# First attention: lead of the maxima, order of the start, place of the shift rows' move and form of the negation

## The reference

```python
q = (x @ Wq.T).reshape(b, t, 8, 64)
kv = x @ Wkv_down.T                                  # latent of 64
k = (kv @ Wk_up.T).reshape(b, t, 8, 64)
v = (kv @ Wv_up.T).reshape(b, t, 8, 64)
scores = einsum('bqhd,bkhd->bhqk', q, k) * 64 ** -0.5
out = einsum('bhqk,bkhd->bqhd', softmax(scores), v).reshape(b, t, 512) @ Wo.T
```

## Time and profile before

| what | value |
|---|---|
| median of 3 runs | 2362.17 us |
| the runs | 2358.39, 2362.17, 2366.94 us |
| the profiled execution, its time | 2364.05 us |
| the profiled execution, its span | 2362.0 us |
| PE busy | 2304.0 us, 98% |
| ACT busy | 1469.0 us, 62% |
| DVE busy | 1381.4 us, 58% |
| POOL busy | 1041.4 us, 44% |

### The profile page before, as it was taken

The page is one execution under the profiler, slowest core; times in us unless marked ns, Lnnn a source line. Parts: engine busy times, 40 slices in busy tenths (PEclk is TensorE's granted clock), DMA queues, the critical chain, the costliest instruction groups (busy, mean ns, idle before and its releaser), DMA issues.

```text
span 2362.0 us, 39370 instructions
## 1 busy us (share of the span) xinstructions
PE 2304.0 (98%) x14921; PEld 1418.0 (60%) x14921; DVE 1381.4 (58%) x2122; ACT 1469.0 (62%) x2049; POOL 1041.4 (44%) x674
## 2 busy tenths in 40 slices
PE   7999999999998999999999999999999999999999
PEld 5445555555545888888888886444344444443688
DVE  5666665666653134222222324889889989899364
ACT  5777777777764344444444443678678778778643
POOL 1776776776775355645645745130000000000354
PEclk9999999999999999999999999999999999999999
DMA  2213213212204456555555556342333333332232
GB/s 62 68 48 99 82 55 100 82 55 90 82 21 139 143 177 195 181 170 196 196 171 190 183 172 185 103 110 75 86 75 68 96 71 70 94 83 48 77 109 80
DMA packets 156840, 259.06 MB, mean 110 GB/s; under 512 B 37004, under 2 KB 97292, under 8 KB 156300
## 3 DMA queue, kind: packets, MB, share of 16 engines
q1 hardware_dynamic: 156652, 256.53, 36.4%
HBM read 206.52 MB, written 60.68 MB: 113 GB/s over the span
## 4 chain that ended last, share of the span: by engine, by line
PE 62%; ACT 2%; DVE 1%; DMA 1%; issue 1%; SPq 1%; POOL 0%; POOLq 0%; DVEq 0%
PE m_R L130 46%; PE m_O L130 11%; PE m_X L130 4%; ACT m_P L1796 1%; DMA m_K<-bounce_k 1%; DVE m_mraw L1948 1%; PE m_X L227 1%; SPq L1654 0%; ACT m_OS L1803 0%; PE m_X L2162 0%; DVE m_ln_x L206 0%; PE m_R L227 0%; DMA inverses<-m_rinv 0%; SPq L1681 0%; DVE m_ln_stat L184 0%
## 5 line engine op out<-in xcount | busy, mean ns | idle before, releaser
L1948 DVE TENSOR_REDUCE m_mraw<-m_R 128x2 f32<-128x1024 f32 x512 | 622.8, 1221 | 72.0 <-PE m_R L130 60.8
L1796 ACT ACTIVATE m_P<-m_R 128x1024 f32<-128x1024 f32 x512 | 523.9, 1025 | 153.0 <-PE m_R L130 152.8
L130 PE MATMUL m_O<-m_P,m_V 128*17 128x256 f32 x4096 | 331.1, 395 | 4.5 <-ACT m_P L1796 2.5
L777 DVE CUSTOM_DVE_ANT_0 a_excess<-a_X,a_excess 128x512 f32<-128x512 f32 x256 | 166.5, 688 | 207.0 <-PE a_X L130 204.8
L943 POOL TENSOR_TENSOR a_accp<-a_accp,a_P 128x1024 f32<-128x1024 f32 x96 | 261.1, 2720 | 14.6 <-ACT a_P L628 5.4
L2053 POOL TENSOR_TENSOR m_act0l<-m_xf,m_act0h 128x512 fp32r<-128x512 f32 x128 | 164.9, 1291 | 209.4 <-ACT m_xf L1858 111.3
L628 ACT ACTIVATE a_P<-a_S 128x1024 f32<-128x1024 f32 x256 | 249.4, 1037 | 8.5 <-PE a_S L130 8.5
L130 PE MATMUL m_R<-m_act0h,wt 128*128 128x512 f32 x640 | 251.3, 393 | 0.0
L130 PE MATMUL a_O<-a_P,a_V 128*64 128x512 f32 x1024 | 251.0, 612 | 0.0
L130 PE MATMUL m_R<-m_act0l,wt 128*128 128x512 f32 x640 | 250.4, 391 | 0.0
L130 PE MATMUL m_R<-m_Q,m_K 64*128 64x512 f32 x800 | 201.3, 499 | 2.3 <-DVE m_mraw L1948 2.0
(11 more groups left out here) (271 smaller groups left out, 4172.6 us busy)
## 6 DMA issues: line engine op xcount, KB each, us to landing
wt<-wcopy SPq DMA_DIRECT2D x176, 512.0 KB, 3.4
m_K<-bounce_k SPq DMA_DIRECT2D x96, 128.0 KB, 5.5
m_ln_x<-x SPq DMA_DIRECT2D x23, 512.0 KB, 4.0
a_tile<-in_L_ffn_tiles SPq DMA_DIRECT2D x22, 512.0 KB, 3.6
wcopy<-in_L_ffn_tiles SPq DMA_DIRECT2D x22, 512.0 KB, 5.0
x<-xres SPq DMA_DIRECT2D x78, 128.0 KB, 2.6
m_Q<-bounce_q SPq DMA_DIRECT2D x150, 64.0 KB, 2.2
xres<-x SPq DMA_DIRECT2D x64, 128.0 KB, 2.7
```

The costliest lines, as they stand in the source:

```text
L130: return pe.eng.matmul(out, lhsT, rhs, start=start, stop=stop, skip_group_check=True)
L777: dve.eng.tensor_tensor_reduce(excess[:, h, :], bank(key), excess[:, h, :], 1.0, LOWEST, ALU.add, ALU.max, mraw[u % 2][:, q, h:h + 1]).the ...
L1796: act.eng.activation(P[h % 4][:, :, :], pair(key)[:, :, :], ACT.Exp, scale=SCALE).then_inc(R.free(key))
L1948: dve.eng.tensor_reduce(mraw[u % 2][:, at, :], pair(key)[:, :, :], AX.X, ALU.max).then_inc(R.free(key))
```

## The change

- AHEAD goes from 6 to 5: ten maxima calls at the start instead of twelve; in the loop, the maxima of a step come one turn later, and one turn more at the end has maxima.
- `rows_at` goes from j = 2 to j = 3. On PE and ACT the rows of the next unit now stand at the head of turn j = 3, ahead of its maxima. On SP `move_rows` stands in turn j = 3 and is the last of the turn: behind `move_inverse` of turn j = 2 and, from unit 6 on, behind the store of turn j = 3.
- The negation of the maxima becomes a `tensor_reduce` over an axis of length one, with `negate`, instead of a `tensor_scalar` by -1.
- At the start, the copies of the query weights (ACT and DVE) stand behind the turned tokens; the halves are copied before the low part of the first query; the maxima begin behind the first query and the halves, with the second query behind n = 1 and the values behind n = 3; the rows and then the differences stand behind all ten maxima.

```diff
@@ -255,7 +255,7 @@
-    NH, NG, NP, AHEAD = 2, 4, 6, 6
+    NH, NG, NP, AHEAD = 2, 4, 6, 5
     SCALE = 64 ** -0.5
     UB = 2 * NG
...
@@ -297,7 +297,7 @@
     def rows_at(u, j):
-        return u + 1 if j == 2 and u + 1 < NU else None
+        return u + 1 if j == 3 and u + 1 < NU else None
     def sums_at(u, j):
...
@@ -333,13 +333,15 @@
         out = [("turn", 0, i % 2, i // 2) for i in range(4)] + [("latent", 0, half) for half in range(2)]
-        out += [("q", 0), ("halves", 0), ("q", 1), ("values", 0)]
-        for n in range(2 * AHEAD):
-            out += [("max", n, h) for h in range(NH)] if n % 2 else []
-            out += [("differ", 0, 1), ("differ", 0, 0), ("rows", 0)] if n == NT - 1 else []
+        out += [("q", 0), ("halves", 0)]
+        for n in range(1, 2 * AHEAD, 2):
+            out += [("max", n, h) for h in range(NH)]
+            out += [("q", 1)] if n == 1 else [("values", 0)] if n == 3 else []
+        out += [("rows", 0)] + [("differ", 0, 1), ("differ", 0, 0)]
         pending = None
         for m, (u, j) in enumerate(turns()):
             n = 2 * (m + AHEAD)
+            out += [("rows", rows_at(u, j))] if rows_at(u, j) else []
             out += [("max", n + i, h) for i in range(2) for h in range(NH)] if n < STEPS else []
             out += [("out", *pending)] if pending else []
...
@@ -347,7 +349,6 @@
             out += [("halves", halves_at(u, j))] if halves_at(u, j) else []
             out += [("values", values_at(u, j))] if values_at(u, j) else []
-            out += [("rows", rows_at(u, j))] if rows_at(u, j) else []
             out += [("differ", *differ_at(u, j))] if differ_at(u, j) else []
             out += [("turn", turn_at(u, j)[0], f, turn_at(u, j)[1]) for f in range(2)] if turn_at(u, j) else []
...
@@ -545,12 +546,12 @@
                 if out_at(u, j):
                     load_residual(*out_at(u, j))
-                if rows_at(u, j):
-                    move_rows(rows_at(u, j))
                 if sums_at(u, j) is not None:
                     move_sums(sums_at(u, j))
                 if j == 2 and u:
                     move_inverse(u - 1)
+                if rows_at(u, j):
+                    move_rows(rows_at(u, j))
             for i in range(3):
                 sp.wait_ge(s_copy, 16 * LOWS0)
...
@@ -654,18 +655,16 @@
             act.eng.activation(wkd[0][:, :, :], raw_d, ACT.Copy).then_inc(s_whi)
             norm.scale_act(act, 0, 0, NT // 2)
+            for i in range(4):
+                norm.turn_act(act, 0, i % 2, i // 2)
             act.wait_ge(s_prod, 1)
             for i in range(2):
...
                     to = wq[0][:, k, :].rearrange("p (g i n) -> p g i n", g=NG, i=2)[:, :, i, :]
                     act.eng.activation(to, psS[i][:, k, 0:256].rearrange("p (g n) -> p g n", g=NG), ACT.Copy).then_inc(s_whi)
-            for i in range(4):
-                norm.turn_act(act, 0, i % 2, i // 2)
             for half in range(2):
                 latent_high(0, half)
-            for u in range(2):
-                query_high(u)
-            keep_values(0)
+            query_high(0)
             def way_high(i):
...
@@ -684,13 +683,18 @@
                 for h in range(NH):
                     surplus(n, h)
-                if n == NT - 2:
-                    for half in (1, 0):
-                        differ_high(0, half)
-                    keep_rows(0)
+                if n == 0:
+                    query_high(1)
+                if n == 2:
+                    keep_values(0)
+            keep_rows(0)
+            for half in (1, 0):
+                differ_high(0, half)
             for m, (u, j) in enumerate(turns()):
                 if out_at(u, j):
                     out_high(*out_at(u, j))
+                if rows_at(u, j):
+                    keep_rows(rows_at(u, j))
                 if 2 * (m + AHEAD) < STEPS:
                     for h in range(NH):
...
@@ -703,8 +707,6 @@
                 if values_at(u, j):
                     keep_values(values_at(u, j))
-                if rows_at(u, j):
-                    keep_rows(rows_at(u, j))
                 if differ_at(u, j):
                     differ_high(*differ_at(u, j))
...
@@ -782,7 +784,8 @@
                     if u:
                         dve.wait_ge(*X.filled(("rows", u - 1)))
-                    dve.eng.tensor_scalar(mneg[:, :, :], mraw[u % 2][:, :, :].rearrange("p q h -> p h q"), -1.0, None, ALU.mult).then_inc(s_max)
+                    halved = mraw[u % 2][:, :, :].rearrange("p q (h k) -> p h q k", k=1)
+                    dve.eng.tensor_reduce(mneg[:, :, :], halved, AX.X, ALU.max, negate=True).then_inc(s_max)
             def add(n):
...
@@ -844,18 +847,17 @@
             dve.eng.tensor_tensor(wkd[1][:, :, :], raw_d, f32(wkd[0][:, :, :]), ALU.subtract).then_inc(s_wlo)
             norm.scale(dve, 0, NT // 2, NT)
+            for i in range(4):
+                norm.turn_dve(dve, 0, i % 2, i // 2)
             for i in range(2):
                 for k in range(2):
...
                     to, hi = [w[:, k, :].rearrange("p (g i n) -> p g i n", g=NG, i=2)[:, :, i, :] for w in (wq[1], f32(wq[0]))]
                     dve.eng.tensor_tensor(to, psS[i][:, k, 0:256].rearrange("p (g n) -> p g n", g=NG), hi, ALU.subtract).then_inc(s_wlo)
-            for i in range(4):
-                norm.turn_dve(dve, 0, i % 2, i // 2)
             for half in range(2):
                 latent_low(0, half)
+            keep_halves(0)
             query_low(0)
-            keep_halves(0)
-            query_low(1)
             def way_low(i):
...
@@ -865,9 +867,10 @@
             for n in range(1, 2 * AHEAD, 2):
                 reduce(n)
-                if n == NT - 1:
-                    for half in (1, 0):
-                        differ_low(0, half)
+                if n == 1:
+                    query_low(1)
+            for half in (1, 0):
+                differ_low(0, half)
             pending = None
             for m, (u, j) in enumerate(turns()):
...
@@ -1125,20 +1128,22 @@
             query(0)
             key_halves(0)
-            query(1)
-            pe.wait_ge(s_identr, 1)
-            values(0)
             for n in range(2 * AHEAD):
                 maxima(n)
-                if n == NT - 1:
-                    for half in (1, 0):
-                        differ(0, half)
-                    max_rows(0)
+                if n == 1:
+                    query(1)
+                if n == 3:
+                    values(0)
+            max_rows(0)
+            for half in (1, 0):
+                differ(0, half)
             pe.wait_ge(s_fill, 7)
             pe.wait_ge(s_excess, 2 * AHEAD)
...
             for m, (u, j) in enumerate(turns()):
                 ahead = 2 * (m + AHEAD)
+                if rows_at(u, j):
+                    max_rows(rows_at(u, j))
                 if ahead < STEPS:
                     maxima(ahead)
...
@@ -1157,8 +1162,6 @@
                 if values_at(u, j):
                     values(values_at(u, j))
-                if rows_at(u, j):
-                    max_rows(rows_at(u, j))
                 if differ_at(u, j):
                     differ(*differ_at(u, j))
...
```

## The result

| | before | after |
|---|---|---|
| median | 2362.0 us (4 runs) | 2390.31 us (4 runs, 2387.22 to 2398.09) |
| ratio of after to before | | 1.0118, 95% interval 1.0098 to 1.0139 |
| the profiled execution | 2364.05 us | 2398.09 us |
| PE waiting for M in the first attention | 0 | 26.5 us, 20 times |
| first score | 39.36 us | 38.42 us |

The change costs 28 us. The profiled execution of after lies 7.8 us above its median; 34.0 us separate it from that of before. From the first to the last exponent of the first attention 684.1 us became 719.3 us, 35.2 more. The start gave back 1.8 us (first exponent at 39.60 instead of 41.36 us), and all that follows the first attention differs by less than 1 us.

What follows compares the result with a forecast made beforehand. PE was taken to bound the first attention's loop, so its waits count in full. Start -3.5, lead of five +0.5, negation +1 and rows' move +17 gave +15 us: 2377 us by the median, range 2358 to 2398.

Steps and rivals of the forecast that it cites:

- What bounds the kernel: First attention's loop: PE busy 40.00 of 40.00 us, so a step counts only if PE waits, then in full.
- The move of the rows: SP's queue in the loop: M lands behind write, spreading and store; PE waits in 19 units, 17 us in all.
- its allowance: 0.1 us added for most of the 19 waiting units, as M's DMAs follow three larger ones; 15.5 becomes 17 us.
- M's own landing: End of SP's chain: M lands 1.7 us after its second issue, by small transfers of 1.4 to 2.7 us.
- the same sum: Per unit, times from the reciprocal's end through SP's queue to M's landing; 1.15 us wait in unit 11, none in 14.
- rival (b): Loop: waits also lower PE's clock; ten of the 19 waits would add 17 us, 2394 us; chance 0.07.
- The start: Before the loop: first score from 39.36 to 36.4 us; 3.5 us gained, from 1 to 6.
- the differences are no longer what is late: Start: differences done on PE by 35.6 us, M there at 36.4 us, so M's own DMAs are late next.
- Negation: DVE in the loop: 0.2 us, freeing 0.9 us a unit worth nothing itself; 1 us lost in units 1 to 4.
- Rival (d): Loop: the tensor_reduce waits for POOL after all, some 10 us more, 2387 us; chance 0.04.
- rival (a): Loop: M is in time and the start decides; 2359 us, up to 2368 with few waits; chance 0.19.
- The sum: Whole kernel: start -3.5, lead of five 0.5, negation 1, move of the rows 17, together +15 us; forecast chance 0.66.

Runs made afterwards that it cites:

- experiment 6: The kernel before with the new tensor_reduce as negation and nothing else; 2362.03 us, ratio 0.9997.
- experiment 4: The changed kernel with the old tensor_scalar as negation; 2399.03 us, ratio 1.0145 to the kernel before.
- experiment 1: The changed kernel with SP's move_inverse in turn j = 3 behind move_rows, so M's DMAs go first; 2365.29 us, ratio 1.0011.
- experiment 2: The kernel before with only SP's move_rows moved to the end of turn j = 3, behind move_inverse and the store; 2399.53 us, ratio 1.0151.
- experiment 3: The changed kernel with the 512 KB weight tile copy issued in turn j = 3 behind move_rows; 2376.66 us, ratio 1.0056.

## Why the prediction was right, and where its sizes were off

**What bounds the kernel: right.** PE had no free time in the loop, and the time that it had to wait there came out in full. DVE's saved 0.9 us a unit was worth nothing that can be told (experiment 6).

**The move of the rows: right in mechanism, place and order of the queue, and too small.** The forecast's waits came to 15.5 us, 17 with its allowance; PE's idle time for M is 26.5 us. The term that was mis-sized is the landing of the inverses' write. The step took each unit's own interval from issue to next issue (2.27 us in unit 11) and moved it 1.2 us forward with the issue. But that interval was no property of the write: its end was fixed by the 512 KB copy ahead of it. Issued earlier, the write lands no earlier with respect to the copy. Where nothing else was in flight the sum was right to 0.2 us: in unit 26 the forecast had a wait of 0.3 us, and the turn grew by 0.2 us. Where there is a copy, units 8, 9 and 10 for example, it had 0.5, 0.6 and 0.7 us and the score came 1.8, 2.3 and 1.0 us later. Units 28 and 30 have no copy, and the turns grew by 1.5 and 2.9 us where the sum gives 0.1 and 1.1: there the write met the packets of the instruction queue, and in unit 30 one more issue, a load's, stood ahead of M. Units 1 to 4 were taken as all but free of waits (0.7 us in all), because way and missing store give them time; they waited 0.97 to 1.57 us each, with the write behind the copy.

M's own landing, for which the prediction had only small transfers of 1.4 to 2.7 us to go by, was well placed at 1.7: in the trace's landings of after it takes 1.6 to 1.9 us from the second issue in 30 of 32 units. The about 2.0 us that the prediction names beside it would have been too long. That M might suffer behind the three larger transfers was the wrong place to put the doubt. The range of waits reached to 34 us only by 0.9 us more for M, which did not come, so that it still held the 26.5 us is in part luck. A slip without weight: for unit 14 the same sum gives 5.85 us, not 6.1.

**The granted clock: rival (b) came in part.** Five waits for M, of 1.3 to 2.5 us, were followed by a stretch at the low level that the kernel before doesn't have there (two of them are shown above); the turns behind them grew by 0.9 to 2.4 us, 7 us in all. The kernel before has its own fall at unit 29 (674 to 681 us), which this execution was spared; the unit's first two turns were 4.3 us shorter. The prediction gave it only as an alternative with ten falls and 17 us; it should have stood in the sum with a few.

**The start: a smaller gain than forecast, for another reason.** Forecast: first score at 36.4 us, set by M's landing; measured 38.42 us. The steps up to the third maximum were met within 0.6 us. But the granted clock fell at 28 us and stayed low to 38 us, through the values, maxima and differences:

```profile
32.00:36.00 4.00, 2.86 (x11) 1.49 (x10) 2.89 (x11) 2.16 (x5) 0.00 (x0) 0.50 0.03 6
36.00:39.00 3.00, 3.00 (x14) 2.04 (x14) 0.76 (x2) 1.35 (x3) 0.00 (x0) 0.62 0.01 1
```

and the differences, which I had done at 35.6 us, ran on PE from 35.07 us to the maxima at 37.93 us, right ahead of the first score:

```profile
35.07 0.58 PE L130 MATMUL a_X<-a_Kh,identr 128*128 128x256 f32 x1 [0.53 <-DVE a_mraw L779]
...
37.93 0.67 PE L130 MATMUL a_X<-wt,a_Qh 64*128 64x512 f32 x2
38.42 0.40 PE L130 MATMUL a_S<-a_Qh,a_Kh 64*128 64x512 f32 x2
```

The step that failed is "the differences are no longer what is late". M landed before them. Against the profile of before this is 0.9 us at the first score; at the first exponent, with the first scores now at the full clock where they had 0.52, 1.8 us. In the six profiled executions with ten calls the first exponent stood at 38.3 to 39.6 us. And the new query weights' place was free, as forecast.

**Negation: right.** 0.16 us in place of 1.09 in the median. Moved to the head of the chain in its old form it would likely have cost something (experiment 4). Rival (d) is out: no negation took over 0.17 us. So is rival (a): M was late.

**The sum.** -3.5 + 0.5 + 1 + 17 was forecast. In the profiled execution it is about -1.8 for the start, 26.5 for PE's idle time on M and some 9, as what is left, for the stretches at the low clock, the restarts behind each wait and small things, less the spared fall: 34.0. By the medians the change costs 28.3 us where 15 were forecast, inside the range.

## What to carry to other kernels

When a wait on a queue is moved, ask what ends each landing behind which the moved thing comes to stand; if it is a larger transfer in flight, issuing the small one earlier bought nothing here, and its duration may not be carried over as a constant. A DMA that feeds the engine which bounds the kernel belongs ahead of every DMA with a landing to wait for on the same issuing engine (experiment 1). And when such a DMA is put last on its queue, each link ahead of it, 0.6 us of one issue among them, is paid in every unit that waits for it; experiment 2 lost as much with the longer lead.

## What the runs showed of the hardware

A 4 KB write took 1.4 us from issue to landing when nothing large was in flight, and up to 3.6 us behind a 512 KB copy, landing in most units 0.15 to 0.2 us after it; with the copy moved the median fell to 1.4 us (experiment 3). The Trainium skill, DMA: Bandwidth & Descriptors, in its section on queues, rings and completion order, gives one reason: the increment of a semaphore lands only after every earlier write of the same DMA engine, across its queues. With that rule the order of the landings agrees. It is not the whole of the delay: in unit 9 the write's own last packet ended 3.0 us behind its issue, in unit 26 1.0 us, and from there to the landing it was 0.6 and 0.4 us. So most of the delay lies in the packets and not in the increment. I had read the rule as an order among small things and left it out.

The same write took 2.6 to 3.4 us with a 16 KB packet of the instruction queue in flight and no large transfer landing near it (units 28 and 30 of the changed kernel, 15, 18 and 19 of experiment 3).

The negation as a VectorE tensor_scalar of 128x8 took 0.17 us with GpSimd at rest. In the loop of the kernel before it took 0.7 to 2.4 us, and each of the 31 ended 0.03 us ahead of the end of a GpSimd instruction; as a tensor_reduce of the same shape it took 0.16 us always.

PE's granted clock fell to the lower level behind waits of 1.3 to 2.5 us in an otherwise busy loop, though not behind all of them: a wait of 2.09 us at 261 us was followed by none, one of 1.31 us at 75.5 us by the stretch at 0.50 shown above.
